# Last layer of a four-layer graph network: the masks of the edge lists made on GpSimd instead of VectorE

## The reference

```python
x = _layernorm(x + _L0_gnn_ref(x, adj, adj, L0_gnn_W, L0_gnn_a))
x = _layernorm(x + _L1_gnn_ref(x, adj, L1_gnn_W, L1_gnn_b))
x = _layernorm(x + _L2_gnn_ref(x, adj, L2_gnn_W, L2_gnn_a))
x = _layernorm(x + _L3_gnn_ref(x, adj, L3_gnn_msg_w, ...))

def _L3_gnn_ref(node_feats, adj, msg_w, msg_b, upd_w, upd_b, ln_w, ln_b):
    s = node_feats @ msg_w[:, :D].T
    d = node_feats @ msg_w[:, D:].T
    messages = gelu(s[:, None, :] + d[None, :, :] + msg_b)
    aggregated = einsum('ijd,ij->id', messages, adj)
    new_feats = concatenate([node_feats, aggregated]) @ upd_w.T + upd_b
    h = gelu(new_feats) + node_feats
    return layernorm(h) * ln_w + ln_b
```

## Time and profile before

| | us |
|---|---|
| timed runs | 707.23 median (706.35, 707.23, 710.11) |
| span of the profiled execution, first to last instruction | 785.9 |
| time of the profiled execution itself | not given beside its span |
| busy over the span: TensorE, VectorE, ScalarE, GpSimd | 445.2, 480.0, 301.0, 333.8 |
| busy from 455 to 786 us: TensorE, VectorE, ScalarE, GpSimd | 112.87, 217.90, 71.09, 175.32 |
| busy from 591.3 to 614.1 us (22.8 us): VectorE, GpSimd | 21.79, 17.25 |

### The profile page before, as it was taken

The page is one execution under the profiler, slowest core; times in us unless marked ns, Lnnn a source line. Parts: engine busy times, 40 slices in busy tenths (PEclk is TensorE's granted clock), DMA queues, the critical chain, the costliest instruction groups (busy, mean ns, idle before and its releaser), DMA issues.

```text
span 785.9 us, 6700 instructions
## 1 busy us (share of the span) xinstructions
PE 445.2 (57%) x1987; PEld 269.0 (34%) x1987; DVE 480.0 (61%) x1457; ACT 301.0 (38%) x363; POOL 333.8 (42%) x492
## 2 busy tenths in 40 slices
PE   4221118999999999999843855304504404405231
PEld 4121113444455655444632734203303303303120
DVE  2419608988946569523454559539849749748564
ACT  3565364458823316995611302203213213213131
POOL 7204502555522126400055356726636736736700
PEclk9555555999999999999865886656757757757655
DMA  8999992999712124990022211211112112111200
GB/s 317 367 424 420 398 324 110 365 398 387 298 71 72 56 72 156 425 374 1 28 73 56 73 44 43 54 30 51 47 37 50 52 32 51 50 33 50 54 8 13
DMA packets 32697, 117.20 MB, mean 149 GB/s; under 512 B 8518, under 2 KB 19636, under 8 KB 23892
## 3 DMA queue, kind: packets, MB, share of 16 engines
q1 hardware_dynamic: 19970, 78.21, 25.3%
q0 software_dynamic: 9952, 38.49, 15.5%
q10 hardware_dynamic: 2734, 0.01, 0.2%
HBM read 111.15 MB, written 5.55 MB: 148 GB/s over the span
## 4 chain that ended last, share of the span: by engine, by line
PE 40%; DVE 25%; DMA 11%; issue 10%; another core or an unknown queue 8%; ACT 3%; SPq 1%; ACTq 0%; DVEq 0%
PE ps L122 38%; DMA ring<-in_adjT_dram 11%; DVE agg L1858 4%; DVE G L1855 3%; DVE G L1843 2%; DVE A L1747 1%; DVE st L1761 1%; DVE M L1725 1%; SPq L842 1%; DVE Mh L1724 1%; DVE t L1779 1%; DVE t L1782 1%; DVE t L1781 1%; DVE yo L1788 1%
## 5 line engine op out<-in xcount | busy, mean ns | idle before, releaser
L939 POOL DMA_INDIRECT G<-near,IX x147 | 140.3, 954 | 44.8 <-issue 44.8
L122 PE MATMUL ps<-ident,agg 128*128 128x128 f32 (+1 forms) x44 | 14.3, 420 | 192.6 <-DVE agg L1858 160.2
L122 PE MATMUL ps<-ring,hwu 128*128 128x512 f32 (+3 forms) x264 | 114.3, 586 | 1.0 <-ACT hwu L1032 1.0
L122 PE MATMUL ps<-ring,xT_s 128*128 128x512 f32 (+1 forms) x264 | 108.0, 553 | 0.0
L1522 DVE FIND_INDEX8 I<-V,rows 128x8 uint32<-128x452 f32 (+1 forms) x132 | 82.1, 627 | 0.0
L939 POOL DMA_INDIRECT Go<-near,IO x44 | 43.6, 990 | 89.7 <-DVE IO L1741 59.5
L1532 DVE MAX8 V<-rows 128x8 f32<-128x452 f32 (+1 forms) x132 | 79.9, 618 | 0.8
L122 PEld LDWEIGHTS ps<-ident,agg 128*128 128x128 f32 (+1 forms) x44 | 9.4, 260 | 198.2 <-DVE agg L1858 162.6
L122 PEld LDWEIGHTS ps<-ring,hwu 128*128 128x128 f32 (+1 forms) x264 | 51.0, 203 | 63.9 <-issue 62.7
L1019 ACT ACTIVATE binT<-ring 128x2708 bf16<-128x2708 f32 (+1 forms) x22 | 53.9, 2459 | 45.2 <-DMA ring<-in_adjT_dram 45.2
L1039 ACT ACTIVATE binT<-ring 128x2708 bf16<-128x2708 f32 (+1 forms) x22 | 53.9, 2456 | 29.5 <-PE ps L122 29.5
(11 more groups left out here) (258 smaller groups left out, 843.9 us busy)
## 6 DMA issues: line engine op xcount, KB each, us to landing
ring<-in_adjT_dram SPq DMA_DIRECT2D x46, 1354.0 KB, 15.5
rows<-in_adj_dram POOLq DMA_DIRECT2D x17, 1354.0 KB, 9.5
rows<-in_adj_dram SPq DMA_DIRECT2D x4, 1354.0 KB, 23.7
G<-near,IX POOLq DMA_INDIRECT x147
xT_s<-in_xT_dram SPq DMA_DIRECT2D x1, 1354.0 KB, 6.3
near<-hwu SPq DMA_DIRECT2D x1, 1344.0 KB
out_dram<-yo SPq DMA_DIRECT2D x21, 64.0 KB
near2f<-hwu SPq DMA_DIRECT2D x5, 256.0 KB
```

The source lines that it names most:

```text
L122: return pe.matmul(dst, lhsT, rhs, start=start, stop=stop, skip_group_check=True)
L939: pool.indirect_dma_start(out=dst, out_offset=None, in_=table, in_offset=bass.IndirectOffsetOnAxis(ap=index, axis=0), engine_sem=o_g).then ...
```

## The change

GpSimd makes the masks of rounds 1 to 10 (blocks 2 to 21) with three instructions for each block: the list position clamped into the row's stretch (maximum, minimum), minus the position itself, compared with zero. Blocks 2 to 5 are made ahead of round 0, after the gathers of layer 2; block n+6 ahead of the seven gathers of block n. For this VectorE turns the end position into the last position and, where a row has no entries, moves the bounds out of reach (three small instructions before its first masks, signalled by `v_bounds`). VectorE keeps `rows_to_list(0)`. TensorE's `lists(g)` waits for `o_M` instead of `v_M` from round 1 on. The gathers no longer count up `o_g`.

```diff
--- before.py
+++ after.py
@@ -306,7 +306,8 @@
         v_max, v_row, v_pos, v_rs, v_mv, v_nm = sem("v_max"), sem("v_row"), sem("v_pos"), sem("v_rs"), sem("v_mv"), sem("v_nm")
         v_rank, v_M, v_list, v_A, v_win, v_x3 = sem("v_rank"), sem("v_M"), sem("v_list"), sem("v_A"), sem("v_win"), sem("v_x3")
         v_h, v_out, v_s, v_pre, v_agg, v_opre = sem("v_h"), sem("v_out"), sem("v_s"), sem("v_pre"), sem("v_agg"), sem("v_opre")
-        o_look, o_ix, o_g = sem("o_look"), sem("o_ix"), sem("o_g")
+        o_look, o_ix = sem("o_look"), sem("o_ix")
+        v_bounds, o_M = sem("v_bounds"), sem("o_M")
         s_bad, s_flag = sem("s_bad"), sem("s_flag")
 
 
@@ -930,14 +931,9 @@
                 pool.affine_select(out=blocks, in_=blocks, compare_op=ALU.is_gt, fill=0.0, base=OWN[h],
                                    pattern=[[0, PAIRS - h]], channel_multiplier=-1).then_inc(k_set, 1)
 
-            def all_begun(so_far):
-
-                if so_far:
-                    pool.wait_ge(o_g, so_far)
-
             def gather(dst, table, index, signal):
                 pool.indirect_dma_start(out=dst, out_offset=None, in_=table,
-                                        in_offset=bass.IndirectOffsetOnAxis(ap=index, axis=0), engine_sem=o_g).then_inc(signal, 16)
+                                        in_offset=bass.IndirectOffsetOnAxis(ap=index, axis=0)).then_inc(signal, 16)
 
 
             for dst, src in [(w2c[:, 0:D], w2), (w2T_s, w2T), (w1T_s[:, :], w1T), (w3c[:, 0:D], wdT),
@@ -985,6 +981,20 @@
                     gather(G2[0:rn(n), n, :], near2f[:, :], WIX[0:rn(n), n:n + 1], s_g[g])
 
 
+            def row_to_list(n):
+
+                if n % 2 == 0 and n // 2 >= MSLOTS // 2:
+                    pool.wait_ge(p_list, n // 2 - MSLOTS // 2 + 2)
+                at = M[:, n % MSLOTS, :]
+                steps = Steps(pool, o_look)
+                steps.base = 9 * NB + 2 * (n - 2)
+                steps.done(pool.tensor_scalar(at, iota[:, :], rank[:, 2, n:n + 1], rank[:, 3, n:n + 1], ALU.max, ALU.min))
+                steps.done(pool.tensor_tensor(at, at, iota[:, :], ALU.subtract))
+                pool.tensor_scalar(at, at, 0.0, None, ALU.is_equal).then_inc(o_M, 1)
+
+            pool.wait_ge(v_bounds, 1)
+            for n in range(2, 6):
+                row_to_list(n)
             pool.wait_ge(s_n3, 16 * len(GROUPS2))
             for g in range(NG3):
                 pool.wait_ge(v_list, g + 1)
@@ -997,6 +1007,8 @@
                         pool.wait_ge(c_d, len(GROUPS2))
                     else:
                         pool.wait_ge(v_agg, n - LEAD3 + 1)
+                    if g + 3 < NG3:
+                        row_to_list(n + 6)
                     for k in range(TOP):
                         gather(G3[0:rn(n), n % QUEUE3, k, :], near3[:, :], IX[0:rn(n), n, k:k + 1], s_g[n % QUEUE3])
 
@@ -1376,9 +1388,11 @@
 
             def lists(g):
 
-                pe.wait_ge(v_M, g + 1)
                 if g:
+                    pe.wait_ge(o_M, 2 * g)
                     pe.wait_ge(v_list, g)
+                else:
+                    pe.wait_ge(v_M, 1)
                 w = LISTED if g else EDGE
                 for k in range(CAP):
                     for i in range(2):
@@ -1699,6 +1713,11 @@
             few.done(dve.tensor_tensor(badv[:, 3, :], rank[:, 3, :], rank[:, 0, :], ALU.subtract))
             few.done(dve.tensor_tensor(more[:, 1, :, :], more[:, 1, :, :], badv[:, 3, :].unsqueeze(2).broadcast_to([P, NB, SEGS * 8]), ALU.add))
             few.done(dve.tensor_tensor(E2[:, :, 2 * SEGS * 8:3 * SEGS * 8], more[:, 1, :, :], more[:, 0, :, :], ALU.mult))
+            few.done(dve.tensor_scalar(rank[:, 4, :], rank[:, 1, :], 0.0, 1.0e6, ALU.is_equal, ALU.mult))
+            few.done(dve.tensor_tensor(rank[:, 2, :], rank[:, 2, :], rank[:, 4, :], ALU.subtract))
+            dve.scalar_tensor_tensor(out=rank[:, 3, :], in0=rank[:, 3, :], scalar=1.0, in1=rank[:, 4, :], op0=ALU.subtract,
+                                     op1=ALU.subtract).then_inc(v_bounds, 1)
+            dve.wait_ge(v_bounds, 1)
 
 
             def normal2(g, first, count):
@@ -1721,7 +1740,7 @@
 
             def rows_to_list(g):
                 for n in (2 * g, 2 * g + 1):
-                    few.done(dve.tensor_scalar(Mh[:, n % 2, :], iota[:, :], rank[:, 3, n:n + 1], None, ALU.is_lt))
+                    few.done(dve.tensor_scalar(Mh[:, n % 2, :], iota[:, :], rank[:, 3, n:n + 1], None, ALU.is_le))
                     last = dve.scalar_tensor_tensor(out=M[:, n % MSLOTS, :], in0=iota[:, :], scalar=rank[:, 2, n:n + 1], in1=Mh[:, n % 2, :],
                                                     op0=ALU.is_ge, op1=ALU.mult)
                 last.then_inc(v_M, 1)
@@ -1860,16 +1879,12 @@
             for q in range(CH):
                 own_parts(q)
             dve.wait_ge(c_d, len(GROUPS2))
-            rows_to_list(1)
-            rows_to_list(2)
             list_to_rows(0)
             take_list(1)
             for g in range(NG3):
                 n, later = pair3(g)
                 listed_before_gelu(g)
                 before_gelu(n)
-                if g + 3 < NG3:
-                    rows_to_list(g + 3)
                 aggregate(n)
                 if g:
                     update(g - 1)
```

## The result

The changed kernel takes **795.8 us** (median of six runs, 795.2 to 797.8), the kernel before 707.4 us (six runs, 706.3 to 710.8). The ratio is 1.123, 95% interval [1.120, 1.126]: 88.4 us slower, where +81.8 was forecast. The profiled execution took 795.96 us, 2.2 us more than its span, so this one can be read as it stands.

What follows compares the result with a forecast made beforehand. GpSimd was taken to set the last layer's pace; 73.3 us for masks in rounds 0 to 7 plus 8.5 us ahead of round 0, all else nothing, gave 707.2 + 81.8 = 789.0 us, range 728 to 815 us.

Steps and rivals of the forecast that it cites:

- Premise: Last layer: GpSimd's gathers set the pace, 22.5 us a round against VectorE's 21.3; long VectorE waits are a disturbance.
- bursts: VectorE's stops in every second last-layer round of the first profile; five longest waits 75.7 us, taken as that execution's disturbance.
- (a): VectorE loses 40 mask instructions, 24.7 us in all; credited as nothing, since GpSimd sets the pace.
- (b): GpSimd's three mask instructions over 128x512: 1.52, 1.26 and 1.52 us with gaps, 4.6 us a block.
- high bound: GpSimd's maximum with minimum at twice the one-operation rate: 2.86 us, a mask block 5.9 us.
- cheap masks: Rival: GpSimd streams one-input mask instructions as fast as it writes; 750 us in all, chance 0.10.
- (c): 16 mask blocks between GpSimd's gathers in rounds 0 to 7, all on the path: 73.3 us.
- (d): Four mask blocks before round 0, 18.3 us, partly covered by GpSimd's table wait (9.8 us): 8.5 us uncovered.
- (e): Three small 128x22 instructions more on VectorE before the first list, 0.2 us each: nothing added.
- (f): TensorE's lists wait for GpSimd's masks instead of VectorE's, and masks for free buffers: nothing added.
- (g): Gathers no longer count up a semaphore when the engine is done: taken as 0, bounds 0 to 0.30 us a gather.
- The rival: Dearer masks: VectorE and GpSimd hold each other up, 0.7 us at each mask instruction; 823 us, chance 0.06.

Runs made afterwards that it cites:

- run 8: The kernel before, unchanged, profiled a second time: 707.4 us, with a span of 705.6 us.
- run 6: The kernel before without the seventh neighbour gather from block 6 on (15 gathers fewer, VectorE's work unchanged): 697.1 us, ratio 0.985.
- run 7: The changed kernel plus VectorE's old masks for the 16 blocks of rounds 0 to 7, written where nobody reads them: 796.6 us, ratio 1.124.
- Run 2: The kernel before with VectorE's masks left out for rounds 5 to 10, all other work kept: 704.5 us beside 707.9, ratio 0.995.
- Run 5: The changed kernel with each GpSimd mask made by two one-operation comparisons and a product: 789.6 us, ratio 1.115.
- run 3: The changed kernel with the masks of blocks 2 to 5, ahead of round 0, back on VectorE: 787.1 us, ratio 1.110.
- run 1: The kernel before with only the gathers' semaphore o_g dropped: 708.2 us beside 707.9, ratio 0.999.

## Why the prediction was right, and where its terms were off

With an undisturbed profile of before (run 8) the 88.2 us between the spans (793.8 and 705.6) can be laid out by GpSimd's round starts:

| stretch | before (run 8) | after | difference |
|---|---|---|---|
| to the first gather of the last layer | 435.4 | 446.6 | +11.1 |
| rounds 0 to 7 | 184.9 | 261.8 | +76.9 |
| rounds 8 and 9 | 45.8 | 45.6 | -0.2 |
| from there to the end | 39.5 | 39.9 | +0.4 |

**Premise (GpSimd sets the pace, bursts are a disturbance).** Right. Run 8 has no bursts; in run 6 time falls with gathers until VectorE's 21.3 us bind; in the profile after, GpSimd waits for nothing in the last layer. One reading was off: the round of the earlier trace rows holds one long gather (1.15 us), not two, the next longest being 0.97; 22.7 against 22.5 us is that one.

**(a) Nothing for VectorE's 24.7 us.** Right in kind: run 7 puts 16 blocks' masks back for +0.8 us, within the noise. Run 2 shows a gain of 3.3 us for 14.8 us of work. The prediction has no term for that: it gave every gather its plain length, and in the traces a gather's length goes with the VectorE instruction that is running as it begins (under run 7).

**(b) The mask block, 4.6 us.** This is the mis-sized term. The block takes 5.04. The price of one operation scaled well from 336 elements to 512, for one input and for two; the step that failed is that maximum with minimum was costed as one operation. It takes 2.09 us in place of 1.52, within the high bound of 2.86. Run 5 shows it: 0.52 us for the second operation with its bound, and 0.07 for a bound read per row in place of a constant. The case of cheap masks is refuted: no one-input instruction over 128x512 took less than 1.49 us. The one-input line rate in "GPSIMD Engine Reference", § 3.1, of the Trainium skill is not borne out by this case: 1.50 us was measured, 2.5 times the prediction's estimate of 0.6 us from that page; the page's figure for two inputs agrees with the 1.27 us.

**(c) 16 blocks in rounds 0 to 7, 73.3 us.** The mechanism is as told; 76.9 us was measured. A masked round is 32.65 us, so a block adds 5.07 us to 22.5, and 16 x (5.07 - 4.58) = +7.8. Against it, rounds 0 to 7 of before are 23.1 us on the mean, not 22.5, since 17 long gathers lie in them, where the change has one: 8 x 0.6 = -4.9. The remaining 0.7 us is mostly the round of that one (33.1 us). The forecast took plain gathers for both; that the two errors partly cancel is luck.

**(d) The front, 8.5 us.** Measured +11.1 between the profiles and 8.7 us by run 3 in the medians. The blocks take 20.1 us in place of 18.3, the cover is 10.3 us where 9.8 was worked out from a disturbed wait, and the rest, 1.2 us, is layer 2: it began 0.6 us later (397.8 for 397.2) and its last gather took 1.51 us for 0.92. Over all the profiles, of kernels with and without the change, that start lies between 396.7 and 399.7 us, so part (e), 0, is neither contradicted nor measured to better than a microsecond or so.

**(f) No wait for masks or mask buffers.** GpSimd's waits show none, and the rounds have their length from its own work.

**(g) The dropped semaphore, 0.** Shown by run 1 to within its noise (ratio 0.997 to 1.002), and the gap is 0.30 us in both.

**Contention.** The rival feared GpSimd's masks held up by VectorE. In the change it goes the other way. Groups of one tile in the change and then in run 7: ns min/median/max, first and last start:

```profile
L991 POOL TENSOR_SCALAR M<-iota,rank x20: 2068/2093/2099, 426.4 to 694.2; 128x512 f32<-128x512 f32 x20
...
L1756 DVE TENSOR_TENSOR Mh<-listed,Mh x11: 557/860/862, 409.0 to 741.6; 128x384 f32<-128x384 f32 x11
```

```profile
L1750 DVE TENSOR_SCALAR Mh<-iota,rank x16: 597/825/1214, 467.5 to 699.1; 128x512 f32<-128x512 f32 x16
```

GpSimd's first mask instruction varies by 31 ns in 2093. VectorE's list instruction takes 0.86 us in the seven rounds in which it meets L993 and 0.56 in the four in which it doesn't; the mask that took 0.48 us in the kernel before takes 0.83 in the median beside GpSimd's, up to 1.21. GpSimd's masks are not untouched in the other runs: the longest in run 7 are 2.24 us for L991 and 1.69 for L993, where the change has 2.10 and 1.51, and in run 5 the product takes up to 1.37 us for 1.27. That is 0.05 to 0.2 us, in ten of the 60 instructions of run 7 and in five of run 5's, beside some 5 us a block, and far from the rival's 0.7 us at every instruction. Here "SBUF — State Buffer", § SBUF: two separate sides, of the Trainium skill names a lock on a shared pair of ports, under which the later of two instructions waits. The rows agree in part. In run 7 the VectorE mask that begins during L992 ends 0.3 us after it, much as one that waits for its end; but the list instruction, which begins 0.16 us after L993, ends 0.48 us before it and so hasn't waited it out. All of it falls into VectorE's 104.3 us of waiting and costs nothing that the time shows.

## What to carry to other kernels

Work moved onto the engine that sets the pace costs its whole duration, and what the other engine is relieved of is worth nothing until the pace changes hands. Find that engine in a profile whose span fits the timed median: where it doesn't, say which waits don't belong, and take a second profile if there is one to be had. On GpSimd, count the operations of an elementwise instruction, not only its elements and inputs. And a difference of a few us between two such kernels may be in the length of the gathers, so count the long ones before explaining it otherwise.

## What the runs showed of the hardware that was not expected

- On GpSimd a second operation, with its own bound per row, in a 128x512 f32 instruction costs 0.52 us (2.09 beside 1.57 us, the profile after and run 5); a comparison with a bound per row in place of a constant takes 0.07 us more (1.57 beside 1.50).
- VectorE instructions grow beside GpSimd's elementwise work (0.56 to 0.86 us, in four cases of run 5 to 1.50; 0.48 to 0.83 us), GpSimd's by 0.05 to 0.2 us, in ten of 60 instructions at most (runs 5 and 7).
- The same gather over 128 rows takes 0.94 us or, in 2 to 18 of 191 cases, 1.07 to 1.45 us. In runs 1 and 8 each long one begins while a certain VectorE instruction is running, and is longer by what that one has left, less 0.12 us. The count changes between kernels whose gathers are the same, and is worth up to 5 us in 707.
- A profiled execution can be 79 us longer than the kernel's timed runs, with stops that no instruction explains and that a second profile of the same kernel doesn't show.
